# Products of two gate halves packed into one PSUM block of a GRU step: half as many columns per matmul, twice as many matmuls

## What is computed

```
def cell(h, x):
    gi = x @ W_ih + b_ih
    gh = h @ W_hh + b_hh
    i_r, i_z, i_n = jnp.split(gi, 3, axis=-1)
    h_r, h_z, h_n = jnp.split(gh, 3, axis=-1)
    r = jax.nn.sigmoid(i_r + h_r)
    z = jax.nn.sigmoid(i_z + h_z)
    n = jnp.tanh(i_n + r * h_n)
    h_new = (1.0 - z) * n + z * h
```

## Time and profile before

| | |
|---|---|
| median of 3 runs | 1900.22 us (1894.44 to 1901.37) |
| profiled execution, first to last instruction | 1898.4 us |
| TensorE matmuls, busy | 1724.2 us, 41087 matmuls |
| TensorE weight loads, busy | 1165.7 us, 41087 loads |
| VectorE, busy | 1297.8 us |
| ScalarE, busy | 779.8 us |
| mean granted TensorE clock | 0.992 |

### The profile page before, as it was taken

The page is one execution under the profiler, slowest core; times in us unless marked ns, Lnnn a source line. Parts: engine busy times, 40 slices in busy tenths (PEclk is TensorE's granted clock), DMA queues, the critical chain, the costliest instruction groups (busy, mean ns, idle before and its releaser), DMA issues.

```text
span 1898.4 us, 95651 instructions
## 1 busy us (share of the span) xinstructions
PE 1724.2 (91%) x41087; PEld 1165.7 (61%) x41087; DVE 1297.8 (68%) x5788; ACT 779.8 (41%) x2714; POOL 300.4 (16%) x600
## 2 busy tenths in 40 slices
PE   6888888878889999989899999989799999988998
PEld 5777677666556666656566666656566666664444
DVE  6888778887667777767676767667677777764323
ACT  5655566543234343423234444432234444323442
POOL 2222222221211110121211111121211111121001
PEclk8999999999999999999999999999999999999999
DMA  7435444444326667425336677426336666439994
GB/s 259 142 144 195 172 166 170 153 187 137 125 89 193 197 209 220 147 86 147 118 89 196 197 215 212 146 72 169 102 104 203 192 202 192 135 91 372 389 357 147
DMA packets 176689, 334.06 MB, mean 176 GB/s; under 512 B 46448, under 2 KB 46600, under 8 KB 176264
## 3 DMA queue, kind: packets, MB, share of 16 engines
q1 hardware_dynamic: 171144, 311.17, 51.1%
q0 software_dynamic: 5120, 16.78, 2.7%
HBM read 263.10 MB, written 64.78 MB: 173 GB/s over the span
## 4 chain that ended last, share of the span: by engine, by line
PE 66%; DVE 16%; ACT 6%; issue 5%; SPq 3%; DMA 2%; another core or an unknown queue 1%; DVEq 0%; POOL 0%; ACTq 0%
PE bank_g L681 15%; PE bank L967 14%; PE bank_g L686 12%; PE bank_g L697 9%; PE bank L987 7%; DVE xt L1439 5%; DVE na L1445 3%; DVE pre L1441 3%; DVE hs_early L1451 3%; ACT seq_h L1113 3%; ACT rz L1113 3%; PE bank L723 2%; PE bank L963 1%; PE bank L949 1%; PE bank_l L973 1%
## 5 line engine op out<-in xcount | busy, mean ns | idle before, releaser
L1841 POOL COPY hxs<-hs 128x32 f16<-128x32 f16 x512 | 223.8, 437 | 1380.8 <-DVE hs L1459 1380.8
L681 PE MATMUL bank_g<-whh,hs_early 128*32 128x256 f16 x8192 | 319.0, 276 | 123.1 <-DVE hs_early L1451 122.1
L1113 ACT ACTIVATE rz<-pre 128x32 f32<-128x32 f32 x512 | 125.9, 246 | 737.2 <-DVE pre L1441 736.3
L1439 DVE STREAM_TRANSPOSE xt<-bank_g 128x256 f32<-128x256 f32 x512 | 231.0, 451 | 212.8 <-PE bank_g L686 198.8
L681 PEld LDWEIGHTS bank_g<-whh,hs_early 128*32 128x32 f16 x8192 | 171.4, 96 | 318.5 <-DVE hs_early L1451 312.9
L697 PE MATMUL bank_g<-whh,hs 128*32 128x128 f16 x16384 | 327.9, 220 | 10.9 <-issue 10.5
L686 PE MATMUL bank_g<-whh,hs 128*32 128x256 f16 x8192 | 314.6, 274 | 0.1
L967 PE MATMUL bank<-wm,wih 128*128 128x512 f16 x1272 | 309.7, 381 | 3.1 <-issue 2.4
L697 PEld LDWEIGHTS bank_g<-whh,hs 128*32 128x32 f16 x16384 | 259.8, 97 | 15.3 <-issue 12.5
L686 PEld LDWEIGHTS bank_g<-whh,hs 128*32 128x32 f16 x8192 | 204.5, 96 | 22.8 <-DVE hs L1459 3.4
L1113 ACT ACTIVATE seq_h<-na 128x16 f32<-128x16 f32 x512 | 114.9, 224 | 237.5 <-DVE na L1445 237.5
(11 more groups left out here) (245 smaller groups left out, 2063.0 us busy)
## 6 DMA issues: line engine op xcount, KB each, us to landing
wm<-moe_split SPq DMA_DIRECT2D x318, 512.0 KB, 4.5
wm<-in_w_moe SPq DMA_DIRECT2D x32, 768.0 KB, 5.4
moe_split<-wm SPq DMA_DIRECT2D x32, 768.0 KB, 5.1
wih<-x_rows SPq DMA_DIRECT2D x58, 256.0 KB, 4.7
y_rows<-wih SPq DMA_DIRECT2D x58, 256.0 KB, 4.6
whh<-moe_split SPq DMA_DIRECT2D x24, 512.0 KB
gi<-moe_split SPq DMA_DIRECT2D x18, 512.0 KB, 6.6
xr<-in_x SPq DMA_DIRECT2D x16, 512.0 KB, 4.1
```

What stands on the lines that cost most here:

```text
L681: mm(out_strip(0, j, 2 * P), early_cols[:, 8 * B * k:8 * B * (k + 1)], strip(whh[:, 1, k, 0:2 * D], j), start=(k == 0), stop=False)
L1113: return nc.scalar.activation(dst, src, func, **kw)
L1439: link(V.transpose(rows, bank_g[0][:, 0:2 * P].rearrange("p (m c) -> p m c", c=32)))
L1841: Q.tensor_copy(hxs[:, par, :, :, :, col].rearrange("p s k b -> p s (k b)"), hs_new).then_inc(S["h_kept"], 1)
```

## The change

For each chunk of the state there are now two sets (`q`) in place of one. Set 0 takes the state's view as it is, set 1 takes a view that begins two columns earlier, so that the high and low parts stand at indices 6 and 7 of a group. Its products fall into rows that set 0 leaves empty. Both sets accumulate into the same PSUM columns: set 0 carries the first half of the weight columns, set 1 the second. The reset and update gates thus take 128 columns of a strip in place of 256, the candidate 64 in place of 128, and VectorE's two transposes read half as many columns. The candidate's bias is multiplied ahead of the step, behind a wait for the semaphore `n_pre` of the step before. The reduction and the sigmoid read or write through other views; their element counts stay the same.

```
             def gru(t):
 
+                if t:
+                    pe.wait_ge(S["n_pre"], t)
+                else:
+                    pe.wait_ge(S["bias_row"], 1)
+                for q in range(SETS):
+                    for j in range(K):
+                        mm(out_strip(1, j, P // SETS), state(bias_to, 0, q), strip(n_cols(bias_n, q), j),
+                           start=(q == 0), stop=False)
                 pe.wait_ge(S["h_hi"], t + 1)
                 for k in range(K):
-                    for j in range(K):
-                        mm(out_strip(0, j, 2 * P), early_cols[:, 8 * B * k:8 * B * (k + 1)],
-                           strip(whh[:, 1, k, 0:2 * D], j), start=(k == 0), stop=False)
+                    for q in range(SETS):
+                        for j in range(K):
+                            mm(out_strip(0, j, SET_COLS // 4), state(early_cols, k, q), strip(of_set(1, k, q), j),
+                               start=(k == 0 and q == 0), stop=False)
...
-                for j in range(K):
-                    mm(out_strip(1, j, P), bias_to[:, :], strip(bias_n[:, :], j), start=True, stop=False)
                 for k in range(K):
                     for w in range(2):
-                        for j in range(K):
-                            i = mm(out_strip(1, j, P), hs_cols[:, 8 * B * k:8 * B * (k + 1)],
-                                   strip(whh[:, w, k, 2 * D:], j), start=False, stop=(k == K - 1 and w == 1))
+                        for q in range(SETS):
+                            for j in range(K):
+                                i = mm(out_strip(1, j, P // SETS), state(hs_cols, k, q), strip(n_cols(whh[:, w, k, 2 * D:], q), j),
+                                       start=False, stop=(k == K - 1 and w == 1 and q == SETS - 1))
...
+        def state(v, k, q):
+
+            return v[:, 8 + 8 * B * k - 2 * q:8 + 8 * B * (k + 1) - 2 * q]
...
                 dve.wait_ge(S["gates_mm"], t * 2 + 1)
-                link(V.transpose(rows, bank_g[0][:, 0:2 * P].rearrange("p (m c) -> p m c", c=32)))
+                link(V.transpose(rows, bank_g[0][:, 0:SET_COLS // 4].rearrange("p (g c) -> p g c", c=32)))
...
-                link(V.transpose(rows_n, bank_g[1][:, 0:P].rearrange("p (g q s) -> p g q s", q=4, s=2)))
+                link(V.transpose(rows_n, bank_g[1][:, 0:P // SETS].rearrange("p (g q s) -> p g q s", q=4, s=2)))
```

More of the change, by code:

```diff
@@ L34 @@
 GROUP = 3
+SETS = 2
+CHUNKS = 2 * K // SETS
+SET_COLS = 2 * D // SETS
 AS, WS = 16.0, 64.0
@@ L683, in gru @@
                 pe.wait_ge(S["h_ready"], t + 1)
                 for k in range(K):
-                    for j in range(K):
-                        i = mm(out_strip(0, j, 2 * P), hs_cols[:, 8 * B * k:8 * B * (k + 1)],
-                               strip(whh[:, 0, k, 0:2 * D], j), start=False, stop=(k == K - 1))
+                    for q in range(SETS):
+                        for j in range(K):
+                            i = mm(out_strip(0, j, SET_COLS // 4), state(hs_cols, k, q), strip(of_set(0, k, q), j),
+                                   start=False, stop=(k == K - 1 and q == SETS - 1))
@@ L688, in gru @@
                 i.then_inc(S["gates_mm"], 1)
                 if t == 0:
-                    pe.wait_ge(S["bias_row"], 1)
                     pe.wait_ge(S["whh_split"], 3)
-                for j in range(K):
-                    mm(out_strip(1, j, P), bias_to[:, :], strip(bias_n[:, :], j), start=True, stop=False)
                 for k in range(K):
                     for w in range(2):
-                        for j in range(K):
-                            i = mm(out_strip(1, j, P), hs_cols[:, 8 * B * k:8 * B * (k + 1)],
-                                   strip(whh[:, w, k, 2 * D:], j), start=False, stop=(k == K - 1 and w == 1))
+                        for q in range(SETS):
+                            for j in range(K):
+                                i = mm(out_strip(1, j, P // SETS), state(hs_cols, k, q), strip(n_cols(whh[:, w, k, 2 * D:], q), j),
+                                       start=False, stop=(k == K - 1 and w == 1 and q == SETS - 1))
@@ L1118, in gates_now @@
                 now = gi[:, col // TB, :, :, col % TB:col % TB + 1]
-                run(ext.unsqueeze(3), now[:, 0:2 * K], ACT.Copy)
+                run(ext, now[:, 0:2 * K, :, 0].rearrange("p (q g) b -> p q g b", q=SETS), ACT.Copy)
                 run(seq_n[:, :, GROUP - 1:GROUP].rearrange("p (k b) o -> p k b o", b=B), now[:, 2 * K:], ACT.Copy
@@ L1124, in gru_rz @@
                 act.wait_ge(S["rz_pre"], t + 1)
-                run(r_new.rearrange("p a o -> p (a o)"), pre[:, :, :].rearrange("p m b -> p (m b)"),
-                    ACT.Sigmoid, scale=1 / PS).then_inc(S["rz_done"], 1)
+                run(rz_new, pre_sets, ACT.Sigmoid, scale=1 / PS).then_inc(S["rz_done"], 1)
             def gru_n(t):
```

39 lines of the change are left out of this document (23 added, 16 removed).

## The result

The changed kernel takes 2745.68 us (median of 4 runs, 2741.74 to 2746.86); the kernel before, on the same chip, 1900.8 us (4 runs). The ratio is 1.4464, with a 95% interval of 1.443 to 1.4498. The forecast was 2205 us with a range up to 2430: the side was right, the time lies 316 us above the range.

The account below looks back on a forecast made before the run. Now bound by the step's latency chain and TensorE work, about equal; after, by instruction fetch: 578 blocks x 3.4 = 1965 us against 1650, +315 on 1898.4, 2213, less 8 for existing stops: 2205 us, range 1930 to 2430.

Parts of the forecast that it names:

- The third bound, instructions: TensorE's instruction fetching, not met before but near, would bind the changed kernel: 578 blocks in place of 306; chance 0.78.
- One block fetched while another runs: TensorE's instruction supply: one block of 256 is fetched while another is run, and no more are held ahead.
- I take the mean as 3.4 us: Fetch time per block, chosen between bounds of 2.4 and 3.37 or 5.5 us; 578 x 3.4 = 1965 us against 1650.
- the 3.37 us pass: Densest pass of 256 TensorE instructions found in the kernel before, without a stop; taken to show one fetch fitted into it.
- It should grow with the load transfers: The delay until a block's packet starts, 3.1 us in the bad pass, less than 1 in the good, grows with SyncE's loads.
- The burst: A step's 272 GRU instructions come within about 1.5 us, so a block border inside exposes most of a fetch.
- The transpose, −0.135 us: Reset and update's transpose falls from 256 to 128 columns, 451 to 316 ns, taking 0.135 us off each step's chain.
- 64 columns, 0.03 us a round: Bias and candidate matmuls at 64 columns: 0.03 us a round between 0.029 and 0.057, eighteen rounds 0.54 us against 0.51.
- The rival of a floor at 0.057: 64-column rounds cost 0.057 us like 128-column ones and the fetch does not bind: about 2060 us, chance 0.06.
- The bias ahead costs nothing in light steps: Where TensorE has spare time (210 steps), the n_pre wait hides the bias; with full TensorE it costs 0.06 us.
- The rival of the hidden fetch: Fetching stays hidden, several blocks under way when asked for faster: 1867 us; decides itself at 2.85 us a block; chance 0.12.
- The granted clock: Final caveat: gaps in TensorE's work might bring its clock down from 0.99, making the time longer; no size given.

Follow-up runs that it names:

- 2: Kernel before with every GRU matmul cut into two of half its columns, results, transposes and order as before: 2761.8 us, ratio 1.4524.
- 3: Changed kernel with the candidate put back to one set of 128 columns and its transpose with it: 2157.28 us, ratio 1.1337.
- 4: Changed kernel with reset and update put back to one set of 256 columns and their transpose with it: 2217.71 us, ratio 1.1669.
- 13: Kernel before plus unused one-column weight loads, 12 ahead of nearly every 512-column matmul, 5 ahead of each 256-column one; 436 packets: 2086.44 us, ratio 1.0993.
- 14: Kernel before plus unused one-column weight loads, 4 ahead of 512-column matmuls and 2 ahead of 256-column ones: 1930.24 us, ratio 1.0165.
- 5: Changed kernel with most expert-weight loads bringing an eighth of their columns, same instructions and number of transfers: 2517.8 us, ratio 1.3561.
- 6: Kernel before with most expert-weight loads bringing an eighth of their columns, same instructions and number of transfers: 1856.26 us, ratio 0.9988.
- 1: Kernel before with only the candidate's four bias matmuls moved ahead of the step, behind the wait for n_pre: 1899.87 us, ratio 0.9996.
- before_spread: The same run as 13, kernel before with 12 or 5 unused loads ahead of wide matmuls: 2086.44 us, ratio 1.0993.

## Why the prediction was right in kind and too low

- **The third bound, instructions.** Right, with its sign. Splitting without packing (2) gives the whole loss, packing's parts (3, 4) and the spread loads (13, 14) follow the number of packets, and the stops are 256 instructions apart. 593 packets were forecast and are there.
- **One block fetched while another runs.** It holds here as stated: the packet of the next block starts 1.83 us (mean) after its predecessor is entered, and its instructions run 2.43 us later. The Trainium skill ("Runtime: NRT & Kernel Launch", section "Instruction fetch mechanics") gives 16 KiB blocks of 256 instructions, as the packets of every run show. "Mostly hidden" agrees with before, at 1650 / 306 = 5.4 us of work a block, and not with the changed kernel, where 499 of 580 passes stop.
- **The failed step: "I take the mean as 3.4 us: the bound of the undisturbed pass, since a part of the passes is far above it."** The term was mis-sized: it measures 4.32 us, and 576 x 4.32 is the whole stretch of 2490 us, against my 578 x 3.4 = 1965. The difference of 525 us is nearly all of the miss. The fastest passes between two stops of the changed kernel take 3.3 us, so what I took for the mean is near the fastest. I had read a fast pass as the usual one and the 5.5 us pass as the exception, though the bounds of 3.37 and 5.5 have 4.4 in their middle. In the changed kernel a value of 3.3 to 3.5 us belongs to passes with hardly any traffic (DMA share 0.02 and 0.03); one at a share of 0.50 takes 4.83 us.
- **Why the 3.37 us pass was no bound.** I wrote "so one fetch fitted into 3.37 us". It ran at a DMA share of 0.56, where the changed kernel's pass at 0.50 takes 4.83 us. It was also no block: counted on from the stop at 1265.40 us by 11 x 256 instructions, a border of blocks falls at about 1327.9, and this block takes some 3.46 us. The next packet starts at 1327.97, within 0.1 us of its first matmul, where no pass between two stops of the changed kernel has less than 1.03 us. So most of the delay lay ahead of the window that I took for the whole of it. My reading, which this one pass supports and no experiment shows: the windows count when instructions run in the array, but a fetch seems to be asked for when TensorE's sequencer enters the block, and a sequencer that was well supplied stands ahead of the array. A starved one has no such lead, so all of the request's delay is exposed.
- **"It should grow with the load transfers".** Right: less data (5) brings the mean delay before the packet from 1.83 to 1.41 us and the ratio from 1.446 to 1.356; for the kernel before (6) it does nothing. I named this and then put no number on it.
- **The burst.** "A border inside it exposes most of a fetch" is seen in the timeline (1.62 and 1.35 us within the low weights) and in the 436-packet kernel, which loses 10%, about two thirds of it in stops, though 436 x 4.32 = 1884 us would about fit into the old time.
- **The transpose, −0.135 us.** Right: 451 to 318 ns, −0.133. It comes to nothing, since the matmuls ahead of it are late.
- **64 columns, 0.03 us a round.** It measures 0.037 us, within its bounds; 0.007 x 16 = 0.11 us a step in a group that is waiting for instructions anyway. The rival of a floor at 0.057 is refuted by the 0.75 us of the timeline.
- **The bias ahead costs nothing in light steps.** Moving it changes nothing in the kernel before (1). What its narrow matmuls cost in the full steps of the changed kernel can't be told beside the stops.
- **The rival of the hidden fetch** needed 2.85 us a block; no stopped pass between two stops is below 3.29.
- **The granted clock.** I named it last as something that would lengthen the time. It fell from 0.992 to 0.937 in the mean. What it added to 2740 us stays open: no run held the clock up with the stops in place, and a pass that waits for its fetch anyway hides slower matmuls, so the clock acts mainly in the 81 passes that end in no stop.

Timeline of TensorE in the changed kernel at one such fall:

```profile
1032.33 1.46 PE L995 MATMUL bank<-wm,wih 128*128 128x512 f16 x6
...
1034.23 0.34 PE L716 MATMUL bank_g<-whh,hs 128*32 128x128 f16 x11
1037.30 0.79 PE L716 MATMUL bank_g<-whh,hs 128*32 128x128 f16 x21 [2.73 <-issue]
1037.78 1.16 PE L725 MATMUL bank_g<-whh,hs 128*32 128x64 f16 x64
1038.87 2.39 PE L995 MATMUL bank<-wm,wih 128*128 128x512 f16 x6
```

Six matmuls of 512 columns take 1.46 us ahead of a stop of 2.73 us and 2.39 us behind it; the candidate's 64 take 1.16 in place of 0.75. Windows of the changed kernel ahead of the stop and behind it:

```profile
1030.00:1034.00 4.00, 3.49 (x163) 2.26 (x153) 1.79 (x10) 1.22 (x5) 0.25 (x2) 1.00 0.39 76
1037.30:1041.20 3.90, 3.90 (x92) 2.31 (x92) 1.84 (x10) 0.73 (x4) 0.33 (x1) 0.56 0.37 141
```

The granted clock went from 1.00 to 0.56, that is from 2.4 GHz to nearly 1.2, after an idle time that the fetch had made.

None of the kernels that compute the same result is faster than the one before. Packing halves columns but doubles instructions, and in this program instructions were the scarcer of the two.

## What to carry to other kernels

In a program that is written out, divide a stage's time by its TensorE instructions / 256 before you split or narrow matmuls, a load counted with each: here 5.4 us of work a block (1650 / 306) hid the fetch almost wholly, 3.9 us (1650 over 306 + 115 blocks, before_spread) already lost 10%, two thirds of it in stops, and with less work still the time became 4.3 us a block. When TensorE is idle inside a group of equal matmuls with "issue" as the reason, count instructions between two stops; a constant 256 is the fetch. Price a shared latency by its mean under the load that it will meet, not by the best pass of a kernel that seldom meets it.

## What the runs showed of the hardware

- The time between entering a block and the next one's packet depends on the data traffic of the core: 1.16 us at 7 GB/s, 2.4 us at 163 GB/s. From the packet's start to the first instruction it is 2.3 to 2.4 us in both. The means over the grouped passes say the same: 1.18 us below 20 GB/s, 2.98 above 180.
- Weight loads of one column follow one another every 13 ns in a heap (85 in 1.11 us) and every 20 ns beside a matmul of 512 columns (12 in 0.24 us), where they take no time of their own. Ahead of the first wide matmul of a step 12 of them cost 0.16 us. They serve to add instructions to a program at a small cost, which has to be told apart from the stops.
- With four strips side by side a round takes 0.11 us at 256 columns ((901.43 - 900.98) / 4 from the earlier trace rows), 0.057 at 128 and 0.037 at 64: the last halving gives 35% and not 50%.
- The same two kernels gave ratios of 1.4464 and 1.4326 on two chips, each with an interval of 0.35 to 0.5%. The kernel before took 1859 us on one chip and 1898 to 1901 us on the others. A difference of 1 or 2% between two such kernels can only be told on one chip.
